# Q projection as a step of its own, a longer score queue and two-bank weight sharing in the down projection of a transformer layer

## The chip, the cores and the metric

The kernel runs on all 8 cores of one Trainium2 chip. Every core works alone on its own 1024 tokens; nothing is exchanged between cores. The metric is the device time of the slowest core, in microseconds (us). A change of less than about 2% either way is taken as no change.

## What is computed

The reference is one transformer layer on x of shape (2, 4096, 4096), cut here to what matters:

```python
xn = layernorm(x)
# multi-query attention: 32 query heads of 128, one shared key and value head, causal, ALiBi
q, k, v = split(xn @ Wqkv)            # q: 32 x 128, k: 128, v: 128
scores  = q @ k.T * 128**-0.5 + slope[h] * (pos_k - pos_q)     # causal
s = softmax(scores) @ v  @ Wo
# gated feed-forward with ternary weights, INTER = 11008
gate = (xn @ Wg.T) * ag
up   = (xn @ Wu.T) * au
out  = ((silu(gate) * up) @ Wd.T) * ad
return x + s * silu(out)
```

## The kernel before

Each core owns eight 128-token slots (`x_own`), chosen so that causal work is equal over the cores. Four stages follow each other, with a barrier of all engines between them (`b_p1`, `b_p2`, `b_p3`).

**Stage 1** normalizes all tokens that the core's queries can see, transposes them with TensorE, and keeps `xn` (own tokens, features on partitions), keys `ktsb` and values `vkm` in SBUF.

**Stage 2, attention.** The queries form two groups X = 0, 1 of four slots (512 tokens). For each head h and group X the keys are walked in tiles of 512 (8 tiles for X = 0, 7 for X = 1), each in two pairs of 128-key blocks. So a head has 30 steps, and a step has N = 512, 384, 256 or 128 query columns (causality removes slots from the later tiles). One step is:
- TensorE: two score products into the PSUM bank pair `2*pb, 2*pb+1` (L537; the pair alternates, and a step waits in `s_stepfree` until VectorE has emptied the pair of two steps earlier);
- VectorE: `usb = slope*rpsb + scores` (L744), which takes the ALiBi and mask term from the table `rpsb` in SBUF;
- ScalarE: `ptb = exp(usb)` (L891); `usb` and `ptb` have three buffers each;
- TensorE, later: two products with the values into an accumulator bank (L472) and two with a column of ones, which give the softmax sum in bank 5 (L478). `emit_attnv` issues these four; `ATT_LAG = 2` says that they are issued two steps behind the scores. They are called the PV products of a step below.

At the end of a group VectorE runs a tail: copy of the accumulator (L683), reciprocal of the sum row (L688), a cast (L691); TensorE later broadcasts the reciprocal with one matmul (L494), and VectorE multiplies (L699, L705), just ahead of the next group's tail. The sum bank is shared, so the first PV product of the next group waits for the reciprocal (`s_zev`). VectorE issues a tail after its work on the third step of the next group.

The query projection (32 chunks of the hidden dimension, weights `wqb` of one head) runs in halves of 512 tokens, `emit_qp_half`: both halves of heads 0 and 1 ahead of the loop, then the halves of head h+2 behind step 8 and step 22 of head h, into bank 7. VectorE copies them to `qtb`, which has two buffers (`emit_qtr`). GpSimd issues the load of the next head's `wqb` when both halves are done, and behind it two DRAM-to-DRAM casts of `Wd` and `Wo` to bfloat16 until all 48 are out. The table `rpsb` comes in four loads on SyncE's queue, and VectorE waits only for the chunk it needs.

**Stage 3** makes gate and up for 86 chunks of INTER; each explicit weight load serves two 512-column matmuls (L573 to L585). Results go to DRAM as `h_d`.

**Stage 4, down and output projection.** Tokens are in two blocks of 512 (`blk`), output columns in four blocks of 1024 (`o2`); oi counts these 8 blocks. In a block the half m = 0 (columns 0 to 511) runs through all 86 chunks of INTER with four token slots each into banks 0 to 3, then m = 1 into banks 4 to 7 (L616). The weights `wdb` come by GpSimd's queue in loads of 4 chunks x 512 columns (512 KB), two buffers per half; a load waits until the load two before it is used up. Then the output projection runs for jo = 0 into banks 0 to 3 and for jo = 1 into banks 4 to 7 (L630), with `wob` loads of 512 KB. VectorE and ScalarE finish each half: `gbuf` (L808), silu (L936), `sgb` (L819), residual add `oeb` (L828), store. VectorE's order is gbuf x4 of the half 0, sgb and oeb x4 of half 0, then the same for half 1. TensorE enters m = 0 of the next block when the first half's four banks are free, and m = 1 when the other four are.

Of the kernel before, what the change touches and what calls it, by code (L numbers as in the profile page):

```python
# [17 lines left out]
NLD = (IC + 3) // 4  # L18
# [8 lines left out]
NG = 15  # L27
# [60 lines left out]
M["usb"] = 176256  # L88
M["ptb"] = 188544
M["atstg"] = 194688  # L90
M["rzbsb"] = M["ag_t"]
assert M["atstg"] + 2048 <= 198624
# [44 lines left out]
def build_nc(dbg=False):  # L137
# [26 lines left out]
    def sb(name, shape, dt):  # L164
# [26 lines left out]
    qtb = sb("qtb", [128, 2, 1024], BF16)  # L191
# [11 lines left out]
            for i in range(4)]  # L203
# [19 lines left out]
                "b_p1", "s_rp", "s_wq", "s_stepdone", "s_stepfree", "s_qpmm", "s_qtr",  # L223
# [5 lines left out]
                "s_wdc", "s_wdc2", "s_woc", "s_dbgd", "s_cvt",  # L229
# [18 lines left out]
    NSH = 30  # L248
# [13 lines left out]
    with nc.Block() as block:  # L262

        @block.sync
        def _(q):
# [37 lines left out]
            for blk in range(2):  # L303
                if blk == 1:
                    q.wait_ge(SM["s_wdc"], 4 * IC)
                    q.wait_ge(SM["s_wdc2"], 4 * IC)
# [8 lines left out]
        def _(g):  # L315
# [22 lines left out]
            g.wait_ge(SM["s_kv"], 2 * NG)  # L338
            g.dma_start(wqb[:, :, :], wq4[0, :, :, :]).then_inc(SM["s_wq"], 16)
# [3 lines left out]
            for h in range(1, NH):  # L343
                g.wait_ge(SM["s_qpmm"], 2 * h)
# [30 lines left out]
            g.wait_ge(SM["s_cvt"], 16 * 48)  # L375
            woL = 0
            def _endicx(L):
                return (L // NLD) * IC + min(4 * (L % NLD) + 4, IC)
            for oi in range(8):
                blk, o2 = oi // 4, oi % 4  # L380
                for m in range(2):
                    cons = "s_wdc" if m == 0 else "s_wdc2"
                    for jj in range(NLD):
                        c = min(4, IC - 4 * jj)
                        L = oi * NLD + jj
                        if L >= 2:
                            g.wait_ge(SM[cons], _endicx(L - 2))
                        src = wdt_bf[4 * jj * 128:(4 * jj + c) * 128,
                                     o2 * 1024 + 512 * m:o2 * 1024 + 512 * m + 512
# [18 lines left out]
        def _(t):  # L408
# [44 lines left out]
            def emit_attnv(d):  # L453
# [5 lines left out]
                if first:  # L459
# [5 lines left out]
                    if g < 2:  # L465
                        t.wait_ge(SM["s_qtr"], 4)
# [558 lines left out]
```

## Time and profile before

| what | value |
|---|---|
| runs | 7837.72, 7880.9, 8567.01 us (median 7880.9) |
| profiled execution, whole | 7926.46 us |
| its span (slowest core, core 2) | 7924.9 us |
| spans of its eight cores | 7796.5 to 7924.9 us |
| TensorE busy | 6558.6 us (83%) |
| VectorE busy | 1948.4 us (25%) |
| ScalarE busy | 1222.4 us (15%) |
| DMA | 841.58 MB, mean 106 GB/s |

Busy shares are means over four stages with different limits. Matmuls are pipelined: a 512-column matmul is listed with 379 ns from start to end, while the next one starts long before that end, so busy times of single lines add up to more than the engine's. The profiled execution has two groups of cores: cores 0 to 3 share one die and ended at 7895 to 7925 us, cores 4 to 7 the other and ended at 7797 to 7831 us, at a higher granted TensorE clock.

### The profile page before, as it was taken

The numbers are of one execution on the slowest core, as the hardware profiler recorded it, in microseconds if no ns is written. First come the engines' busy times: TensorE is split into PE (matmuls) and PEld (weight loads), VectorE is DVE, ScalarE is ACT, GpSimd is POOL, SyncE is SP. The second block draws the span as 40 slices with busy tenths as digits, with TensorE's granted clock in tenths as the row PEclk, the third lists the DMA queues.
The fourth block names the chain that finished last, engine by engine and source line by source line (L and its number), as shares of the span: only waits on it lengthen the run. The fifth ranks groups of instructions, "written<-read, shape, count | busy, mean of one in ns | idle before, by whom it ended". The sixth has DMA issues, their size and how long they took to land.

```text
span 7924.9 us, 103467 instructions; the slowest of 8 cores (7796.5 to 7924.9 us)
## 1 busy us (share of the span) xinstructions
PE 6558.6 (83%) x29648; PEld 3574.2 (45%) x50512; DVE 1948.4 (25%) x2460; ACT 1222.4 (15%) x1931; POOL 533.2 (7%) x811
## 2 busy tenths in 40 slices
PE   4665657777777777999999999999677888888988
PEld 2333333444444333455555555555344544444544
DVE  5545525555555556000000000000000000000000
ACT  3333313333333333000000000000000000000000
POOL 0000000000000000000000000000111111111111
PEclk9666678888888888999999999999899987777877
DMA  5333388777755110444444444444443434433333
GB/s 181 149 128 138 138 129 110 109 109 108 105 87 85 21 21 12 85 91 85 81 86 86 90 86 85 85 85 86 159 134 122 134 127 162 139 126 115 124 127 116
DMA packets 244517, 841.58 MB, mean 106 GB/s; under 512 B 108306, under 2 KB 116516, under 8 KB 193360
## 3 DMA queue, kind: packets, MB, share of 16 engines
q0 software_dynamic: 113712, 658.76, 38.0%
q1 hardware_dynamic: 111904, 142.63, 5.8%
q10 hardware_dynamic: 18432, 33.56, 1.2%
q8 instruction: 340, 5.57, 0.3%
q14 instruction: 129, 1.06, 0.0%
HBM read 1126.93 MB, written 171.44 MB: 164 GB/s over the span
## 4 chain that ended last, share of the span: by engine, by line
PE 67%; DMA 14%; DVE 10%; issue 4%; ACT 4%; ACTq 0%; DVEq 0%; SPq 0%; POOL 0%; POOLq 0%
PE P L616 10%; DMA wdb<-wdt_bf 8%; PE P L574 8%; PE P L577 8%; PE P L585 7%; PE P L582 7%; PE P L507 6%; PE P L630 4%; PE P L472 4%; PE P L478 4%; PE P L537 3%; PE P L432 3%; DMA wob<-wo_bf 3%; DVE rzrow L688 3%; DVE usb L744 3%
## 5 line engine op out<-in xcount | busy, mean ns | idle before, releaser
L616 PE MATMUL P<-wdb,hblk 128*128 128x512 bf16 x5504 | 1400.9, 418 | 188.0 <-DMA wdb<-wdt_bf 144.4
L574 PE MATMUL P<-xn,wgb 128*128 128x512 bf16 x2752 | 1044.1, 379 | 12.0 <-DMA wub<-wu 12.0
L577 PE MATMUL P<-xn,wgb 128*128 128x512 bf16 x2752 | 1044.0, 379 | 0.0
L582 PE MATMUL P<-xn,wub 128*128 128x512 bf16 x2752 | 1043.0, 379 | 0.0
L585 PE MATMUL P<-xn,wub 128*128 128x512 bf16 x2752 | 1043.0, 379 | 0.0
L744 DVE SCALAR_TENSOR_TENSOR usb<-rpsb,P 128x768 f32<-128x768 f32 (+3 forms) x960 | 763.1, 795 | 874.9 <-PE P L537 740.6
L615 PEld LDWEIGHTS <-hblk 128*128 128x128 bf16 x5504 | 566.2, 105 | 811.9 <-issue 321.2
L891 ACT ACTIVATE ptb<-usb 128x768 bf16<-128x768 f32 (+3 forms) x960 | 686.5, 715 | 1447.7 <-DVE usb L744 1370.9
L472 PE MATMUL P<-ptb,vkm 128*128 128x128 bf16 (+3 forms) x1920 | 468.0, 328 | 423.5 <-DVE rzrow L688 400.2
L630 PE MATMUL P<-wob,atblk 128*128 128x512 bf16 x2048 | 546.7, 433 | 182.0 <-DVE gbuf L808 111.6
L417 PE MATMUL P<-I_bf,xntok 128*128 128x128 bf16 x2176 | 347.8, 265 | 384.5 <-DVE xntok L664 319.9
L783 DVE SCALAR_TENSOR_TENSOR hstg<-P,au_t,sgs 128x512 bf16<-128x512 f32 x86 | 64.6, 751 | 2271.3 <-ACT sgs L906 2271.3
L616 PEld LDWEIGHTS P<-wdb,hblk 128*128 128x128 bf16 x5504 | 519.8, 96 | 0.0
L507 PE MATMUL P<-xn,wqb 128*128 128x512 bf16 x2048 | 460.4, 384 | 58.0 <-DMA wqb<-wq 58.0
L537 PE MATMUL P<-qtb,ktsb 128*128 128x128 bf16 (+3 forms) x1920 | 441.0, 313 | 35.6 <-DVE usb L744 35.4
L417 PEld LDWEIGHTS P<-I_bf,xntok 128*128 128x128 bf16 x2176 | 225.4, 104 | 506.4 <-issue 461.5
L478 PE MATMUL P<-ptb,ones_bf 128*1 128x128 bf16 (+3 forms) x1920 | 441.7, 313 | 0.0
L573 PEld LDWEIGHTS <-wgb 128*128 128x128 bf16 x2752 | 269.5, 98 | 337.5 <-issue 13.5
L471 PEld LDWEIGHTS <-vkm 128*128 128x128 bf16 x1920 | 175.8, 102 | 544.8 <-issue 506.9
L581 PEld LDWEIGHTS <-wub 128*128 128x128 bf16 x2752 | 269.3, 98 | 324.7
L629 PEld LDWEIGHTS <-atblk 128*128 128x128 bf16 x2048 | 217.1, 108 | 431.3 <-issue 257.2
L903 ACT ACTIVATE sgs<-P,ag_t 128x512 f32<-128x512 f32 x86 | 59.2, 688 | 2239.4 <-PE P L585 2239.4
(76 smaller groups left out, 4947.3 us busy)
## 6 DMA issues: line engine op xcount, KB each, us to landing
wdb<-wdt_bf POOLq DMA_DIRECT2D x336, 512.0 KB, 3.8
wdt_bf<-wdt POOLq DMA_DIRECT2D x32, 2752.0 KB, 52.3
wgb<-wg POOLq DMA_DIRECT2D x86, 1024.0 KB, 8.4
wub<-wu POOLq DMA_DIRECT2D x86, 1024.0 KB, 12.8
wob<-wo_bf POOLq DMA_DIRECT2D x128, 512.0 KB, 4.2
xtile<-x_cov SPq DMA_DIRECT2D x60, 1024.0 KB, 5.4
xtile<-x_cov POOLq DMA_DIRECT2D x60, 1024.0 KB, 7.5
wqb<-wq POOLq DMA_DIRECT2D x32, 1024.0 KB, 12.1
```

The lines of the kernel that those rows point to most:

```text
L472: t.matmul(P[:, ab, co:co + N], vkm[:, (kcb + ci) * 128:(kcb + ci + 1) * 128], ptb[:, ub, j, 0:N], start=(first and j == 0), stop=(last an ...
L478: ins = t.matmul(P[0:1, 5, co:co + N], ones_bf[:, 0:1], ptb[:, ub, j, 0:N], start=(first and j == 0), stop=(last and j == 1))
L507: ins = t.matmul(P[:, bk, :], wqb[:, cc, :], xn[:, cc * 1024 + 512 * half: cc * 1024 + 512 * half + 512], start=(cc == 0), stop=(cc == HC ...
L537: ins = t.matmul(P[:, 2 * pb + j, 0:N], ktsb[:, kcol + ci * 128: kcol + (ci + 1) * 128], qtb[:, h % 2, qoff:qoff + N], start=True, stop=True)
L574: t.matmul(P[:, pg0, :], wgb[:, i % 2, cc, :], xn[:, cc * 1024:cc * 1024 + 512], start=(cc == 0), stop=(cc == HC - 1))
L577: t.matmul(P[:, pg1, :], wgb[:, i % 2, cc, :], xn[:, cc * 1024 + 512:(cc + 1) * 1024], start=(cc == 0), stop=(cc == HC - 1))
L582: t.matmul(P[:, pu0, :], wub[:, i % 2, cc, :], xn[:, cc * 1024:cc * 1024 + 512], start=(cc == 0), stop=(cc == HC - 1))
L585: ins = t.matmul(P[:, pu1, :], wub[:, i % 2, cc, :], xn[:, cc * 1024 + 512:(cc + 1) * 1024], start=(cc == 0), stop=(cc == HC - 1))
L616: ins = t.matmul(P[:, sl + 4 * m, :], hblk[sl][:, icx, :], wdb[:, slot, :], start=(icx == 0), stop=(icx == IC - 1))
L630: ins = t.matmul(P[:, sl + 4 * jo, :], atblk[:, hcx, sl * 128:(sl + 1) * 128], wob[:, slot, :], start=(hcx == 0), stop=(hcx == HC - 1))
L744: ins = v.scalar_tensor_tensor(usb[:, ub, :, 0:N], rpsb[:, o:o + 2 * N].rearrange("p (a b) -> p a b", b=N), float(SLOPES[h]), P[:, 2 * pb: ...
L891: ins = s.activation(ptb[:, ubp, :, 0:N], usb[:, ubu, :, 0:N], AF.Exp)
```

## The change

1. **Query projection.** It becomes a step ("qp", h) of the step list, ahead of each head's 30 steps. One explicit weight load serves both 512-column matmuls, into the bank pair of that step. VectorE empties both banks in one instruction into a single `qtb`; the first score step of the head waits for that. Heads 0 and 1 are no longer projected ahead, and no half stands inside a head. The first `wqb` load is issued behind the stage barrier, not ahead of it; the load of head h+1 is issued when the projection of head h is done.
2. **`ATT_LAG`** goes from 2 to 3; the broadcast matmul uses bank 7 and `rzbsb` gets its own place.
3. **`rpsb`** comes in one load, and VectorE waits for all of it before anything else of the stage.
4. **Down projection.** The loop over m is gone: one explicit weight load serves two matmuls (columns 0 to 511 and 512 to 1023), all eight banks are in use, and `wdb` loads hold 4 chunks x 1024 columns (1 MB), two buffers. A block starts when all eight banks of the block before are free. VectorE's order is unchanged.

The core of the diff:

```diff
+        steps.append(("qp", h))
...
-            for ck in range(4):
-                q.dma_start(rpsb[:, ck * 4608:(ck + 1) * 4608],
-                            rp[:, ck * 4608:(ck + 1) * 4608]
-                            ).then_inc(SM[f"s_wd{4 + ck}"], 16)
+            q.dma_start(rpsb[:], rp[:, :]).then_inc(SM["s_rp"], 16)
...
-            g.wait_ge(SM["s_kv"], 2 * NG)
-            g.dma_start(wqb[:, :, :], wq4[0, :, :, :]).then_inc(SM["s_wq"], 16)
             g.wait_ge(SM["s_xn"], NT)
             g.nop().then_inc(SM["b_p1"], 1)
             g.wait_ge(SM["b_p1"], 4)
-            for h in range(1, NH):
-                g.wait_ge(SM["s_qpmm"], 2 * h)
+            nsteph = 1 + 2 * (NKT[0] + NKT[1])
+            for h in range(NH):
+                if h >= 1:
+                    g.wait_ge(SM["s_stepdone"], nsteph * (h - 1) + 1)
                 g.dma_start(wqb[:, :, :], wq4[h, :, :, :]).then_inc(SM["s_wq"], 16)
...
+                for j in range((IC + 3) // 4):
+                    c = min(4, IC - 4 * j)
+                    t0 = 2 * IC * oi + 8 * j
+                    if oi > 0 and j < 2:
+                        g.wait_ge(SM["s_wdc"], 2 * IC * oi)
+                    elif j >= 2:
+                        g.wait_ge(SM["s_wdc"], t0 - 8)
+                    src = wdt_bf[4 * j * 128:(4 * j + c) * 128,
+                                 o2 * 1024:(o2 + 1) * 1024].rearrange(
+                                     "(a p) (m n) -> p a m n", p=128, n=512)
+                    g.dma_start(wdb[:, 8 * (j % 2):8 * (j % 2) + 2 * c, :]
+                                .rearrange("p (a m) n -> p a m n", m=2), src
+                                ).then_inc(SM[f"s_wd{wdL % 2}"], 16)
...
-            ATT_LAG = 2
+            ATT_LAG = 3
...
+                if stp[0] == "qp":
+                    h = stp[1]
+                    t.wait_ge(SM["s_wq"], 16 * (h + 1))
+                    for cc in range(HC):
+                        t.ldweights(wqb[:, cc, :])
+                        t.matmul(P[:, 2 * pb, :], wqb[:, cc, :],
+                                 xn[:, cc * 1024:cc * 1024 + 512],
+                                 start=(cc == 0), stop=(cc == HC - 1))
+                        ins = t.matmul(P[:, 2 * pb + 1, :], wqb[:, cc, :],
+                                       xn[:, cc * 1024 + 512:(cc + 1) * 1024],
+                                       start=(cc == 0), stop=(cc == HC - 1))
+                    ins.then_inc(SM["s_stepdone"], 1)
...
+                    if first and X == 0:
+                        t.wait_ge(SM["s_stepfree"], si)
...
-                for m in range(2):
-                    if oi == 0 and m == 0:
-                        t.wait_ge(SM["s_adb"], 8)
-                    if oi > 0:
-                        t.wait_ge(SM["s_gb"], (oi - 1) * 8 + 4 * (m + 1))
-                        t.wait_ge(SM["s_sgb"], (oi - 1) * 8 + 4 * (m + 1))
...
+                if oi == 0:
+                    t.wait_ge(SM["s_adb"], 8)
+                else:
+                    t.wait_ge(SM["s_gb"], oi * 8)
+                    t.wait_ge(SM["s_sgb"], oi * 8)
+                for icx in range(IC):
+                    L = oi * 22 + icx // 4
+                    slot = 8 * ((icx // 4) % 2) + 2 * (icx % 4)
+                    t.wait_ge(SM[f"s_wd{L % 2}"], 16 * (L // 2 + 1))
+                    for sl in range(4):
+                        t.ldweights(hblk[sl][:, icx, :])
+                        for j in (0, 1):
+                            ins = t.matmul(P[:, sl + 4 * j, :], hblk[sl][:, icx, :],
+                                           wdb[:, slot + j, :],
+                                           start=(icx == 0), stop=(icx == IC - 1))
...
+            v.wait_ge(SM["s_rp"], 16)
...
+                if stp[0] == "qp":
+                    h = stp[1]
+                    v.wait_ge(SM["s_stepdone"], si + 1)
+                    tv.wait_self(v)
+                    ins = v.tensor_scalar(
+                        qtb[:, :].rearrange("p (a b) -> p a b", a=2),
+                        P[:, 2 * (si % 2):2 * (si % 2) + 2, :],
+                        SCALE, None, ALU.mult)
+                    tv.inc(ins, SM, "s_stepfree", 1)
```

## Rows read from the trace of the kernel before

**Rows 1.** Span and mean granted TensorE clock of one core.

```profile
core 7: 7830.8 us, clock 0.908
```

**Rows 2.** Busy time by window, core 4: window, length, engines, clock, DMA share, GB/s.

```profile
3196.00:5560.00 2364.00, 2358.62 (x10929) 1283.90 (x16389) 121.25 (x172) 110.25 (x173) 88.90 (x168) 1.00 0.43 85
5628.00:7925.00 2297.00, 1715.45 (x7503) 1015.80 (x15002) 132.88 (x192) 40.40 (x64) 357.02 (x476) 0.96 0.38 128
```

**Rows 3.** Waits of core 4: who waited for whom, total us, times, longest.

```profile
PE P L472 <- DVE rzrow L688: 400.2, 63, 6.8
PE P L616 <- DMA wdb<-wdt_bf: 218.7, 187, 3.3
PE P L630 <- DVE gbuf L808: 111.1, 8, 14.5
```

**Rows 4.** Timeline of TensorE, core 4, start of attention: start, length, what, idle before.

```profile
1030.86 15.37 PE L507 MATMUL P<-xn,wqb 128*128 128x512 bf16 x64 [10.59 <-DMA wqb<-wq]
1063.28 16.21 PE L507 MATMUL P<-xn,wqb 128*128 128x512 bf16 x64 [17.05 <-DMA wqb<-wq]
...
1120.74 9.59 PE L507 MATMUL P<-xn,wqb 128*128 128x512 bf16 x32 [27.71 <-DMA wqb<-wq]
```

**Rows 5.** Timeline of TensorE, core 2, one head of attention.

```profile
2201.94 7.08 PE L507 MATMUL P<-xn,wqb 128*128 128x512 bf16 x32
...
2215.28 0.61 PE L537 MATMUL P<-qtb,ktsb 128*128 128x512 bf16 x2
...
2224.41 1.03 PE L472 MATMUL P<-ptb,vkm 128*128 128x512 bf16 x2 [6.29 <-DVE rzrow L688]
...
2231.59 0.50 PE L537 MATMUL P<-qtb,ktsb 128*128 128x384 bf16 x2
...
2232.81 0.50 PE L537 MATMUL P<-qtb,ktsb 128*128 128x384 bf16 x2
...
2248.89 0.60 PE L537 MATMUL P<-qtb,ktsb 128*128 128x512 bf16 x2
...
2258.45 1.04 PE L472 MATMUL P<-ptb,vkm 128*128 128x512 bf16 x2 [6.41 <-DVE rzrow L688]
...
2266.47 0.82 PE L507 MATMUL P<-xn,wqb 128*128 128x512 bf16 x3
```

**Rows 6.** Timeline of VectorE, core 2, in the same head.

```profile
2220.90 3.35 DVE L688 RECIPROCAL rzrow<-P 1x512 f32<-1x512 f32 x1
...
2225.66 1.22 DVE L744 SCALAR_TENSOR_TENSOR usb<-rpsb,P 128x1024 f32<-128x1024 f32 x1
```

**Rows 7.** Timeline of TensorE, core 4, down and output projection.

```profile
5613.73 9.07 PE L616 MATMUL P<-wdb,hblk 128*128 128x512 bf16 x32 [29.15 <-DMA atblk<-at_d]
5624.03 7.18 PE L616 MATMUL P<-wdb,hblk 128*128 128x512 bf16 x32 [1.24 <-DMA wdb<-wdt_bf]
5632.12 3.63 PE L616 MATMUL P<-wdb,hblk 128*128 128x512 bf16 x16 [0.91 <-DMA wdb<-wdt_bf]
...
5699.54 8.77 PE L616 MATMUL P<-wdb,hblk 128*128 128x512 bf16 x32 [1.98 <-DMA wdb<-wdt_bf]
...
5799.99 7.07 PE L630 MATMUL P<-wob,atblk 128*128 128x512 bf16 x32
...
6151.36 7.07 PE L616 MATMUL P<-wdb,hblk 128*128 128x512 bf16 x32
```

**Rows 8.** DMA issues, core 2: what, queue, count, KB each, median us to landing.

```profile
wdb<-wdt_bf POOLq DMA_DIRECT2D x336, 512.0 KB, 3.8
...
wdb<-wdt_bf POOLq DMA_DIRECT2D x16, 256.0 KB, 3.3
```

**Rows 9.** Timeline of VectorE, core 4, around the ends of projections.

```profile
5711.73 1.49 DVE L808 TENSOR_TENSOR gbuf<-P,adb 128x512 f32<-128x512 f32 x2 [0.15 <-DVE gbuf L808]
...
6156.67 0.69 DVE L819 SCALAR_TENSOR_TENSOR sgb<-P,g2buf 128x512 f32<-128x512 f32 x1
```

**Rows 10.** Timeline of TensorE, core 2, late in stage 4.

```profile
7041.39 8.58 PE L630 MATMUL P<-wob,atblk 128*128 128x512 bf16 x32 [1.19 <-DMA wob<-wo_bf]
```

More of the change, by code:

```diff
@@ L87 @@
 M["qtb"] = 172160
[L88 to L92, printed above, removed]
+M["usb"] = 174208
+M["ptb"] = 186496
+M["atstg"] = 192640
+M["rzbsb"] = 194688
+assert M["rzbsb"] + 2048 <= 198624
 M["wgb"] = 90240
@@ L190, in build_nc @@
     wqb = sb("wqb", [128, HC, 128], BF16)
-    qtb = sb("qtb", [128, 2, 1024], BF16)
+    qtb = sb("qtb", [128, 1024], BF16)
     usb = sb("usb", [128, 3, 2, 512], F32)
@@ L247, in build_nc @@
     NSTEP = len(steps)
-    NSH = 30
     pair_idx = {}
@@ L493, in emit_tail_mm @@
                     t.wait_ge(SM["s_rzb"], tg)
-                ins = t.matmul(P[:, 4 + 2 * (tg % 2), :], ones_bf[0:1, :],
-                               rzbf[0:1, tX, :], start=True, stop=True)
+                ins = t.matmul(P[:, 7, :], ones_bf[0:1, :], rzbf[0:1, tX, :],
+                               start=True, stop=True)
                 ins.then_inc(SM["s_rzmm"], 1)
@@ L498, in emit_tail_mm @@
                 return ins
-            def emit_qp_half(j, half):
-                t.wait_ge(SM["s_wq"], 16 * (j + 1))
-                if j >= 2:
-                    t.wait_ge(SM["s_qtr"], 2 * j + half)
-                bk = 7 if j >= 2 else (0, 1, 4, 5)[2 * j + half]
-                for cc in range(HC):
-                    t.ldweights(wqb[:, cc, :])
-                    ins = t.matmul(P[:, bk, :], wqb[:, cc, :],
-                                   xn[:, cc * 1024 + 512 * half:
-                                      cc * 1024 + 512 * half + 512],
-                                   start=(cc == 0), stop=(cc == HC - 1))
-                ins.then_inc(SM["s_qpmm"], 1)
-            for j in range(2):
-                for half in range(2):
-                    emit_qp_half(j, half)
             for si, stp in enumerate(steps):
@@ L534, in _ @@
-                for j in (0, 1):
-                    ci = 2 * pr + j
-                    t.ldweights(ktsb[:, kcol + ci * 128: kcol + (ci + 1) * 128])
-                    ins = t.matmul(P[:, 2 * pb + j, 0:N],
-                                   ktsb[:, kcol + ci * 128: kcol + (ci + 1) * 128],
-                                   qtb[:, h % 2, qoff:qoff + N],
-                                   start=True, stop=True)
-                ins.then_inc(SM["s_stepdone"], 1)
-                if tail is not None and si > tail_armed + 8:
-                    emit_tail_mm()
@@ new lines, in _ @@
+            for si, stp in enumerate(steps):
+                if stp[0] == "qp":
[7 more added lines that the diff above has]
+                    tv.inc(ins, SM, "s_stepfree", 1)
+                else:
+                    _, h, X, kt, pr = stp
+                    lo, ns = CFG[X][kt]
+                    N = ns * 128
+                    first = (kt == 0 and pr == 0)
+                    last = (kt == NKT[X] - 1 and pr == 1)
+                    pb = si % 2
+                    ub = pr_cnt2 % 3
+                    o = RP_OFF[(X, kt)] + 2 * pr * N
+                    v.wait_ge(SM["s_stepdone"], si + 1)
+                    if pr_cnt2 >= 3:
+                        v.wait_ge(SM["s_pt"], pr_cnt2 - 2)
+                    tv.wait_self(v)
+                    ins = v.scalar_tensor_tensor(
+                        usb[:, ub, :, 0:N],
+                        rpsb[:, o:o + 2 * N].rearrange("p (a b) -> p a b", b=N),
+                        float(SLOPES[h]), P[:, 2 * pb:2 * pb + 2, 0:N],
+                        ALU.mult, ALU.add)
+                    tv.inc(ins, SM, "s_stepfree", 1)
+                    pr_cnt2 += 1
+                    if last:
+                        pend_t.append((h, X, pair_idx[(h, X, kt, pr)]))
+                    while pend_t and pend_t[0][2] + 2 < pr_cnt2:
+                        while pend_t2:
+                            emit_tail_v2(pend_t2.pop(0))
+                        emit_tail_v(pend_t.pop(0))
```

142 lines of the change are left out of this document (38 added, 104 removed).

## The prediction

> **What bounds the kernel now.** I read the spans of the cores first. The slowest core of the profile (core 2, 7924.9 us) is on a die with a lower TensorE clock; the slowest of the other die ends at 7830.8 [rows 1]. Most rows below are of core 4, on that second die. The windows by stage come next [rows 2]. Stage 3 has it busy without a gap, at clock 1.00: 2364 us for 86 x 128 = 11008 matmuls, 0.2148 us each. The change does not touch stage 3. Stage 4 has 1715 of 2297 us busy. VectorE is busy for 133 and ScalarE for 40 of these, so TensorE's work plus its waits make this stage. In attention VectorE matters too, by one chain in each group, shown below. The waits [rows 3] name them: in attention 63 waits for the reciprocal, in stage 4 187 waits for `wdb` and 8 for `gbuf`. A listed wait begins only at the modelled end of the last matmul, about 0.16 us after its last column, so the true gaps are longer; below I take starts from the timelines.
>
> **Start of attention.** Stage 1 ends at 1020.3 on core 4 (the first wait of [rows 4] counts back to it). Before: two projections, then the first score at 1079.3, that is 59.0 us (the second projection, 16.21 us less 0.16 of the last matmul's drain, ends there); then 27.7 us of waiting for `wqb` of head 2 [rows 4]. After: `wqb` of head 0 is issued about 1 us later than stage 1 ends, beside the 9.4 MB of `rpsb` and two casts. Nearest row: the second `wqb` load, issued at the end of the first projection (1046.8) beside the same traffic, let TensorE start at 1063.3, 16.5 us later. So the projection starts near 1038 and ends near 1054. VectorE then waits for all of `rpsb`. Its four loads had landed 39 us after their issue before, with the casts beside them only for the last third; I take 50 us, so the first score is at about 1072: 52 us. The bounds are 42 us (as fast as before, then one eviction) and 67 us (twice as slow as alone). `wqb` of head 1 is issued at 1054 and needed about 64 us later; the slowest one took 40.4 us before. The 27.7 us wait goes. Sum: 59.0 + 27.7 against 52.
>
> **A head of attention.** Before, 64.5 us (2201.94 to 2266.47, [rows 5]). Its parts:
> - two halves of the projection, 32 x 0.2162 = 6.92 us each;
> - twice the chain from the first score of a new group to its first PV product, 2215.28 to 2224.41 = 9.1 us and 2248.89 to 2258.45 = 9.6 us. VectorE sets it: two score evictions of 1.22, the multiply of the group before, the copy, the reciprocal of 3.35 [rows 6];
> - what lies between: 2224.41 to 2248.89 less a half = 17.6 us, and the other 14.4 us.
>
> After:
> - The projection is one block of 64 matmuls in stage 3's pattern, 64 x 0.2148 = 13.75 us, against 13.84.
> - Nothing hides the eviction of `qtb`: the next score waits for it. A 1024-column eviction took 1.22 us [rows 6]; with semaphores 1.5 us. It is bounded by 1.4, and by 3.2 if the clock drops behind the gap (32 matmuls took 8.77 instead of 7.1 us behind a 1.98 us gap, [rows 7]). VectorE loses two copies of 0.69 in exchange, one of which stood in the chain of 9.6; that chain becomes 9.1.
> - The chain itself stays: VectorE's list in it is the same. But TensorE does one more score product and one more old PV step in its shadow, because the queue is one deeper. I added up the stretch between two chains by columns: 512 columns take 0.2148 us, so the six products of a step take 0.97 us at N = 384, and a step without a wait took 2231.59 to 2232.81 = 1.22 us [rows 5], 0.25 more for changing weights. That makes a PV step 1.1, 0.9, 0.7 and 0.5 us and a score pair 0.4, 0.3, 0.2 and 0.1 us for N = 512, 384, 256, 128, plus 1.9 us because the first products behind the chain run at half speed (1.03 us for two, against 0.60). The part of 17.6 us becomes 15.6, that of 14.4 becomes 12.7. About half of this is the step in the shadow, the other half the small waits of TensorE for `ptb` at N = 128, where the scores of two steps ago are barely through VectorE and ScalarE when they are wanted.
> - Could a third pending step hurt? `ptb` has three buffers, so exp of step n waits for PV of n-3, which is issued right behind score n and ends before VectorE is through with score n. No.
>
> Head after: 15.6 + 9.1 + 12.7 + 13.75 + 1.5 + 9.0 = 61.7 us, 2.8 less. If the deeper queue brings nothing it is 65.4. The last two heads had no projection before, one fewer is inside the stage now. Whole stage before: 59.0 + 27.7 + 60 x 6.92 + 32 x 50.7 = 2124 us. After: 52 + 32 x 46.4 + 31 x 15.25 = 2010. **Attention: -114 us** (bounds -124, with the first score 42 us behind stage 1, and +15, with 67 us and the 65.4 us head).
>
> The loads for the casts keep their place: a pair of casts and one `wqb` fill most of the DMA time of a head, and there is about 45 us of slack for `wqb`.
>
> **Down projection.** A block's L616 part on core 4 lasts from 5613.73 to 5799.99 = 186.3 us [rows 7]; the eight add up to 1464. The products alone would take 688 x 0.2148 = 147.8 us. The difference is the `wdb` wait. 16 matmuls use up a load in 3.46 us, but the next into that buffer needs 0.7 us to be issued and 3.9 us to land: 4.6 us. So every second load is late: 5624.03 to 5632.12 is 8.1 us for 32 matmuls. After, a load of 1 MB serves 32 matmuls, 6.9 us. Its landing time is not in the trace. From 256 to 512 KB it rose from 3.3 to 3.8 [rows 8]; two more such steps give 4.8 to 5.1 us, and with 0.8 us for the issue 5.9 us, under 6.9. Upper bound: twice 3.9, then each turn is 8.6 us and 64 matmuls take 15.5 us, where they took 16.2. I take the first, with 4 us in a block for the clock behind its start and for a late load: 152 us. **-248 us** (bounds -265 and -60).
>
> The Trainium skill (DMA: Bandwidth & Descriptors, Anatomy of one DMA) puts a transfer from GpSimd's queue at about 2.0 us plus its bytes at 436 GB/s. By it, as an estimate, doubling 512 KB adds 1.2 us, which is what the two sizes of [rows 8] give too; nothing in the sum rests on it.
>
> What the eight shared banks cost:
> - jo = 0 must wait until banks 0 to 3 are emptied, which lay under m = 1 before. Four `gbuf` take 2 x 1.49 + 0.15 = 3.13 us [rows 9]; the first can start about 1.2 us ahead of the last matmul's end, so 2 us remain, 3 with the clock. 8 x 3 = +24 us.
> - The next block must wait for the fourth `sgb` of jo = 1. TensorE moved on at 6151.36 before [rows 7], that `sgb` ended at 6156.67 + 0.69 = 6157.36 [rows 9]: +6.0 us, 6.3 with the semaphores, at 7 boundaries, one of which already waits 14 us for `atblk`. 6 x 6.3 = +38 us.
> - The 14 us wait ahead of jo = 1 (111 us in all) stays: VectorE still does sgb and oeb of half 0 first.
>
> **Down and output projection: -186 us.**
>
> **Sum.** -114 - 186 = -300. On the second die 7830.8 + 1.6 becomes 7532. On core 2 the last five blocks run at a lower clock (32 matmuls in 8.58 us, 0.268 each, [rows 10]); its waits for `wdb` are shorter, so it gains 98 + 51 instead of 248 there, and 7926.5 becomes about 7725. The median of the runs, 7880.9, is 49 us above the first of these bases. I forecast the undisturbed case with a part of that excess: 7570 us.
>
> **Rivals.**
> - *The denser stage 4 draws a lower clock on both dies.* For it: core 2 did its last blocks at 0.268 us per matmul on the same work. Against: stage 3 is denser than anything in stage 4 and had clock 1.00, core 4 kept 0.96. Price: 8 x (184.4 + 4) = 1507 instead of 1216 us (+291), and the output projection's turns 8.9 instead of 8.1 us for 32 matmuls, 64 of them (+50). 7532 + 341 = 7870: no change. Chance 0.15. The Trainium skill (TensorE: Matmul & The Clock Gate, The HAM clock gate) states a limit that can hold a whole die at 13/16 of the full clock, which speaks for this rival. The trace agrees in size on core 2 (0.2148 / 0.268 = 0.80) and not in stage 3, where core 4 had 1.00 [rows 2].
> - *The 1 MB loads are late too.* At the upper bound -60 instead of -248: 7570 + 188 = 7760. For it: landings scatter, one wait was 3.3 us. Chance 0.09.
> - *The deeper queue brings nothing*, because VectorE's chain decides. Then the head is 65.4 us and attention is unchanged: 7570 + 115 = 7685. Chance 0.12.
> - *Slower: the serial projection starves VectorE and ScalarE.* If with the queue drained each head refilled so slowly that the time behind the projection grew, the loss would be 31 times that. To end 2% above 7880.9 it must eat 458 us, 14.8 us a head; the whole chain of a new group is 9.1 us and is in my sum. Chance 0.04.
>
> **Chances.** Forecast 0.60. Range: its own 7480 to 7660; up to 7790 it takes in the idle queue and the late loads, and part of the lower clock. Faster by over 2% (below 7723): the forecast, the idle queue, and a third of the late loads, 0.75; same 0.20; slower 0.05. Two per cent is about what a measurement of this kernel can tell from no change.
>
> **What would show it.** Waits for `wdb` fall from 219 [rows 3] to under 50 us; the L616 part of a block is near 152 us; TensorE waits about 6 us at seven block starts and 2 us ahead of jo = 0; a head takes 62 us, with a 1.5 us gap behind 64 projection matmuls; the first score is near 1072. The forecast falls if a 1 MB load needs over 7 us from buffer free to landed, or if the clock in stage 4 is near 0.8 on all cores.

## The result, and the profile after

| what | value |
|---|---|
| kernel after, median of 10 runs | 7609.78 us (7588.80 to 8129.08) |
| kernel before, median of its 10 runs beside them | 8361.5 us (7837.72 to 8579.37) |
| ratio after to before | 0.9667, interval 0.9629 to 0.9705 |
| profiled execution, whole | 7610.64 us |
| forecast, as a ratio | 7570 / 7880.9 = 0.9605 |

The median of before is high because in many of its runs the cores of a die were held at a lower TensorE clock; the ratio leaves such runs of both kernels out, and everything below goes by it. Of the kernel before it rests on two times only, 7837.72 and 7880.9 us. So the change gives 3.3%, some 260 us of 7837.72, and not the 752 us between the medians. I had forecast 3.9%, just outside the interval. The time itself is 40 us above the forecast.

The spans by core of the kernel after (its slowest core is 0 now, and the granted clocks of the two dies agree; [rows 1] of before is core 7):

```profile
core 0: 7609.1 us, clock 0.897
...
core 3: 7527.4 us, clock 0.904
core 4: 7568.4 us, clock 0.901
...
core 7: 7596.3 us, clock 0.898
```

Windows of core 4, with the columns of [rows 2]: a stretch of stage 3, and stage 4.

```profile
3160.00:5520.00 2360.00, 2348.57 (x10882) 1278.44 (x16320) 121.22 (x172) 110.23 (x173) 90.97 (x171) 1.00 0.44 85
5569.00:7568.00 1999.00, 1706.36 (x7552) 934.80 (x12352) 132.87 (x192) 40.37 (x64) 226.53 (x302) 0.94 0.43 148
```

Waits of core 4, and the last line of core 0 (who waited for whom, total, times, longest):

```profile
PE P L464 <- DVE rzrow L673: 332.4, 63, 11.6
PE P L615 <- DVE gbuf L781: 124.3, 16, 14.6
PE P L615 <- DMA wob<-wo_bf: 99.0, 60, 12.4
PE P L526 <- DVE qtb L699: 64.4, 32, 15.9
PE P L601 <- DVE sgb L792: 53.2, 7, 15.4
...
DVE atstg L668 <- DMA at_d<-atstg: 16.8, 3, 6.6
PE P L601 <- DMA wdb<-wdt_bf: 6.1, 9, 1.1
```

```profile
DVE atstg L668 <- DMA at_d<-atstg: 47.7, 10, 8.7
```

Three things against [rows 3]. The 218.7 us of waiting for `wdb` are 6.1. The wait for the reciprocal fell from 400.2 to 332.4, though its longest rose from 6.8 to 11.6. And there is a wait that before did not have: VectorE's copy into `atstg` waits for the store of an earlier attention output. It is 47.7 us on core 0 and 6.0 on core 3, and the order of the eight cores by this wait (3, 5, 2, 4, 6, 1, 7, 0) is their order by span. The spans differ by 82 us and the waits by 42, so the wait is not all that sets them apart.

From the last transpose of stage 1 to the end of the last `usb`, core 4 took 2130.2 us before and takes 2079.4 now; core 0 takes 2113.4, core 3 2062.3. So **attention gave 51 us on core 4**, where I had written 114. From the first product of the down projection to the last of the output projection core 4 took 2173.8 us and takes 1989.9: **184 us**, where I had written 186.

The start of attention on TensorE and VectorE (timelines of core 4; compare [rows 4]):

```profile
1023.64 0.38 PE L433 MATMUL P<-I_bf,vtstg 128*128 128x128 bf16 x4 [1.58 <-ACT vtstg L842]
1053.92 0.61 PE L502 MATMUL P<-xn,wqb 128*128 128x512 bf16 x1 [29.90 <-DMA wqb<-wq]
```

```profile
1084.75 1.23 DVE L699 TENSOR_SCALAR qtb<-P 128x1024 bf16<-128x1024 f32 x1 [86.99 <-DMA rpsb<-rp]
```

The first projection starts 30 us behind the last transpose and is over by 1067.7; `rpsb` is all there only at 1084.75, so `rpsb` alone sets the start. A head in the middle of attention (TensorE, then VectorE, core 4; compare [rows 5, 6]):

```profile
2044.91 0.60 PE L526 MATMUL P<-qtb,ktsb 128*128 128x512 bf16 x2 [1.56 <-DVE qtb L699]
...
2054.04 1.03 PE L464 MATMUL P<-ptb,vkm 128*128 128x512 bf16 x2 [4.97 <-DVE rzrow L673]
...
2070.40 0.60 PE L526 MATMUL P<-qtb,ktsb 128*128 128x512 bf16 x2
...
2079.54 1.03 PE L464 MATMUL P<-ptb,vkm 128*128 128x512 bf16 x2 [5.08 <-DVE rzrow L673]
...
2092.27 0.39 PE L502 MATMUL P<-xn,wqb 128*128 128x512 bf16 x1
...
2107.82 0.61 PE L526 MATMUL P<-qtb,ktsb 128*128 128x512 bf16 x2 [1.56 <-DVE qtb L699]
...
2116.95 1.03 PE L464 MATMUL P<-ptb,vkm 128*128 128x512 bf16 x2 [4.97 <-DVE rzrow L673]
...
2132.60 0.60 PE L526 MATMUL P<-qtb,ktsb 128*128 128x512 bf16 x2
...
2141.83 1.03 PE L464 MATMUL P<-ptb,vkm 128*128 128x512 bf16 x2 [5.17 <-DVE rzrow L673]
...
2155.71 0.39 PE L502 MATMUL P<-xn,wqb 128*128 128x512 bf16 x1
```

```profile
2106.43 1.23 DVE L699 TENSOR_SCALAR qtb<-P 128x1024 bf16<-128x1024 f32 x1 [13.79 <-PE P L505]
```

In the order of the forecast this head is 9.13 + 16.36 + 9.14 + 12.73 + 13.75 + 1.80 = 62.9 us, and the next one 63.4.

A block of stage 4 (TensorE, core 4; compare [rows 7]):

```profile
5970.65 7.08 PE L615 MATMUL P<-wob,atblk 128*128 128x512 bf16 x32 [2.19 <-DVE gbuf L781]
...
6018.40 8.63 PE L615 MATMUL P<-wob,atblk 128*128 128x512 bf16 x32 [12.88 <-DVE gbuf L781]
...
6060.86 16.49 PE L601 MATMUL P<-wdb,hblk 128*128 128x512 bf16 x64 [6.52 <-DVE sgb L792]
```

The L601 part of this block had begun at 5814.71 and its products ended near 5968.3: 153.6 us. The eight parts of core 4 take 150.2 to 153.7 us, 152.1 on average, where those of before took 180 to 189, 183 on average. From this block's start to the next it is 246.1 us.

### The profile page after: what moved, and what is told of

It is laid out like the page before. It is cut to its first block, busy times and chain, and to the rows that moved or that the text cites. A ratio compares the mean times of both kernels' runs of the same rounds, so it can differ in the third digit from the quotient of the medians.

```text
span 7609.1 us, 97882 instructions; the slowest of 8 cores (7527.4 to 7609.1 us)
## 1 busy us (share of the span) xinstructions
PE 6257.2 (82%) x29119; PEld 3394.6 (45%) x46736; DVE 1943.1 (26%) x2428; ACT 1222.2 (16%) x1931; POOL 399.8 (5%) x635
## 4 chain that ended last, share of the span: by engine, by line
PE 72%; DMA 10%; DVE 9%; issue 4%; ACT 3%; another core or an unknown queue 1%; ACTq 0%; DVEq 0%; SPq 0%; POOL 0%; POOLq 0%
PE P L601 15%; PE P L562 8%; PE P L570 8%; PE P L559 8%; PE P L567 7%; PE P L615 4%; DMA at_d<-atstg 4%; PE P L470 4%; PE P L526 3%; PE P L464 3%; PE P L427 3%; DMA wob<-wo_bf 3%; PE P L505 3%; PE P L412 3%; PE P L502 3%
## 5 line engine op out<-in xcount | busy, mean ns | idle before, releaser
L601 PE MATMUL P<-wdb,hblk 128*128 128x512 bf16 x5394 | 1201.9, 382 | 97.2 <-DVE sgb L792 55.3
L562 PE MATMUL P<-xn,wgb 128*128 128x512 bf16 x2752 | 1044.3, 379 | 17.1 <-DMA wub<-wu 11.3
L570 PE MATMUL P<-xn,wub 128*128 128x512 bf16 x2752 | 1043.0, 379 | 5.8
L559 PE MATMUL P<-xn,wgb 128*128 128x512 bf16 x2642 | 1002.4, 379 | 0.0
L567 PE MATMUL P<-xn,wub 128*128 128x512 bf16 x2641 | 1000.9, 379 | 0.0
L615 PE MATMUL P<-wob,atblk 128*128 128x512 bf16 x2007 | 489.7, 401 | 234.6 <-DVE gbuf L781 127.4
L601 PEld LDWEIGHTS P<-wdb,hblk 128*128 128x128 bf16 x5504 | 531.4, 97 | 217.9 <-issue 7.6
L599 PEld LDWEIGHTS <-hblk 128*128 128x128 bf16 x2752 | 271.1, 99 | 434.1 <-issue 119.2
L558 PEld LDWEIGHTS <-wgb 128*128 128x128 bf16 x2752 | 269.3, 98 | 336.8 <-issue 12.6
L505 PE MATMUL P<-xn,wqb 128*128 128x512 bf16 x1024 | 389.6, 380 | 8.0 <-issue 6.3
L502 PE MATMUL P<-xn,wqb 128*128 128x512 bf16 x961 | 365.8, 381 | 29.5 <-DMA wqb<-wq 29.5
## 6 DMA issues: line engine op xcount, KB each, us to landing
wub<-wu POOLq DMA_DIRECT2D x86, 1024.0 KB, 13.5
```

Source lines behind the costliest of these rows:

```text
L559: t.matmul(P[:, pg0, :], wgb[:, i % 2, cc, :], xn[:, cc * 1024:cc * 1024 + 512], start=(cc == 0), stop=(cc == HC - 1))
L562: t.matmul(P[:, pg1, :], wgb[:, i % 2, cc, :], xn[:, cc * 1024 + 512:(cc + 1) * 1024], start=(cc == 0), stop=(cc == HC - 1))
L567: t.matmul(P[:, pu0, :], wub[:, i % 2, cc, :], xn[:, cc * 1024:cc * 1024 + 512], start=(cc == 0), stop=(cc == HC - 1))
L570: ins = t.matmul(P[:, pu1, :], wub[:, i % 2, cc, :], xn[:, cc * 1024 + 512:(cc + 1) * 1024], start=(cc == 0), stop=(cc == HC - 1))
L601: ins = t.matmul(P[:, sl + 4 * j, :], hblk[sl][:, icx, :], wdb[:, slot + j, :], start=(icx == 0), stop=(icx == IC - 1))
L615: ins = t.matmul(P[:, sl + 4 * jo, :], atblk[:, hcx, sl * 128:(sl + 1) * 128], wob[:, slot, :], start=(hcx == 0), stop=(hcx == HC - 1))
```

## The experiments

My theory on the result: the down projection did what was forecast, since a load now serves 6.9 us of products instead of 3.46; attention gained less because the first loads collide with the casts, because the half-speed stretch behind each chain is longer than I had allowed, and because the stores of the attention outputs are late. The main rivals: the gain of stage 4 comes from something other than the loads (half as many weight changes, say), and the longer queue does nothing.

**The two halves of the change alone.** `e1_down` is the kernel before with the new down projection only, `e2_att` the kernel before with the new attention only.

> The kernel before with only the down projection changed (shared weight loads, eight banks, 1 MB loads). If the gain of the change is mostly there, as the traces say (core 4: 2173.8 to 1989.9 us for this stage), this gains about 184 us, ratio about 0.977, and its attention stage takes as long as before. If the two parts help each other (a shorter attention stage shifting the clock or the memory traffic of the last stage), it gains clearly less than 184 us.

> The kernel before with only the attention stage changed. Forecast from the prediction: -114 us. From the trace of the changed kernel: about -50 us on core 4, and less on the cores where the stores of at_d come late. Ratio about 0.993 to 0.997. Down projection blocks stay at 180 to 186 us for their L616 part.

Down alone: 0.9815 (0.9649 to 0.9982), the fastest run 7636.91 us against 7827.79 of the kernel before beside it; waits for `wdb` 13.5 us. The interval is wide, but the rows say the same as above:

```profile
6152.39 97.87 PE L615 MATMUL P<-wdb,hblk 128*128 128x512 bf16 x439 [6.14 <-DVE sgb L818]
6306.19 7.08 PE L629 MATMUL P<-wob,atblk 128*128 128x512 bf16 x32 [2.19 <-DVE gbuf L807]
```

153.8 us from one to the other. Attention alone: 0.994 (0.9892 to 0.9988), that is 47 us of 7830. With intervals this wide the two ratios cannot show that the halves leave each other alone; the stages of core 4 can. The down and output projection takes 1990.0 us in `e1_down` and 1989.9 in the kernel after, 2177.4 in `e2_att` and 2173.8 before. Attention takes 2082 us in `e2_att` against 2079 after, and 2139 in `e1_down` against 2130 before. So neither half helps or harms the other by more than 9 us, and the missing part of the forecast is attention's.

**Is it the size of the loads?** `e7_small` is the kernel after with loads of 512 KB (two chunks of 1024 columns) into two buffers. Weight changes, banks and order stay those of after.

```
-                for j in range((IC + 3) // 4):       # loads of 4 chunks, 1 MB
+                for j in range(IC // 2):             # loads of 2 chunks, 512 KB
-                    slot = 8 * ((icx // 4) % 2) + 2 * (icx % 4)
+                    slot = 4 * (L % 2) + 2 * (icx % 2)
```

> The changed kernel with down loads of 2 chunks x 1024 columns (512 KB, two buffers of that size) in place of 1 MB; the shared weight loads and the eight banks stay. If the size of what two buffers hold is what the change gained, every second load is late again: 8.1 us for 32 matmuls, the L601 part of a block goes from 153.6 back to about 180 us and the kernel is 200 to 230 us slower. If sharing the weight loads is the gain (rival), the part stays near 155 us.

Measured: 1.0068 (1.0039 to 1.0097) to the kernel before. From core 4's waits and timeline of TensorE:

```profile
PE P L600 <- DMA wdb<-wdt_bf: 249.7, 226, 3.6
```

```profile
5855.98 9.30 PE L600 MATMUL P<-wdb,hblk 128*128 128x512 bf16 x32 [6.11 <-DVE sgb L791]
...
6041.50 8.71 PE L614 MATMUL P<-wob,atblk 128*128 128x512 bf16 x32 [2.20 <-DVE gbuf L780]
```

The part of this block is 183.3 us again, and that is the shortest of the eight: they take 183.3 to 193.5 us, 189 on average, against 183 before and 152 after. So the size of what the two buffers hold is what the change gained, and the loss is larger than the 200 to 230 us that I had expected: the stage takes 2274.7 us on core 4, 285 more than in the kernel after and 101 more than before. Of these 101, 55 are the two bank waits of the rows, which the forecast had booked, and 51 are parts that are 6 us longer than those of before, with loads of the same size and the same turn; why, no run here shows. 101 less attention's 47 (2082.5 against 2129.9 us) is the loss of 0.7%. Sharing the explicit weight loads gives no time where loads are late; what it could give where none is late, the next run shows.

**Or the depth?** `e8_ring` is the kernel before, half by half, 512 KB loads, but its 2 + 2 buffers used as one ring of four.

```
-                        g.dma_start(wdb[:, 8 * m + 4 * (L % 2):
-                                        8 * m + 4 * (L % 2) + c, :], src
-                                    ).then_inc(SM[f"s_wd{2 * m + L % 2}"], 16)
+                        g.dma_start(wdb[:, 4 * (R % 4):4 * (R % 4) + c, :], src
+                                    ).then_inc(SM[f"s_wd{R % 4}"], 16)
```

> The kernel before with its 512 KB loads, its half after half order and the same 16 KB of wdb a partition, but as one ring of four buffers instead of two for each half, so that a load has three loads' time (10.4 us) instead of one (3.46 us). By the theory that a load is late because of its turn of 4.6 us and not because of its size, the L616 part of a block falls from 182 to about 150 us with no wait for shared banks: -250 us, ratio about 0.968. If small loads are themselves the limit (rival), it stays above 170 us.

Measured: 0.9651 (0.962 to 0.9681). No wait for `wdb` is left in the list, and the part is 148.5 us long in six of the eight blocks and 150 to 151 in the two behind the waits for `atblk` (timeline of TensorE, core 0):

```profile
6076.27 148.66 PE L618 MATMUL P<-wdb,hblk 128*128 128x512 bf16 x688
6224.77 7.07 PE L632 MATMUL P<-wob,atblk 128*128 128x512 bf16 x32
```

688 x 0.2148 is 147.8, so TensorE is full here, with an explicit weight load for every single matmul. By the rate of stage 3, sharing one between two could take off 0.7 us a block at most, and the rival on weight changes falls. (The profile also lists a weight load inside each matmul: stage 4 has 15002 of both kinds for 7503 matmuls in [rows 2] and 12352 for 7552 now, so sharing removed a quarter of those of the down projection and not half.) The median landing of a load was 4.3 us (core 0), longer than the 3.8 of [rows 8], and did no harm. The wait of before came from this: of its four buffers only two were in turn, so a freed one had the 3.46 us of the other to be filled again, where issue and landing need 4.6. In the ring it has three times 3.46. These few lines give as much as the whole change, without its two bank waits.

**The first loads of attention.** `e6_start` is the kernel after with `wqb` of head 0 loaded ahead of stage 1's end and `rpsb` in four loads, as before.

```
+            g.wait_ge(SM["s_kv"], 2 * NG)
+            g.dma_start(wqb[:, :, :], wq4[0, :, :, :]).then_inc(SM["s_wq"], 16)
             g.wait_ge(SM["s_xn"], NT)
-            q.dma_start(rpsb[:], rp[:, :]).then_inc(SM["s_rp"], 16)
+            for ck in range(4):
+                q.dma_start(rpsb[:, ck * 4608:(ck + 1) * 4608], ...)
```

> The changed kernel with the start of attention as before: the first wqb load issued ahead of the barrier and rpsb in four loads, of which VectorE waits for the one it needs. In the changed kernel the first score came 62.6 us behind stage 1 on core 4 (the prediction had 52). If the two late loads are the cause, the first score comes at 27 to 35 us and the kernel gains 25 to 30 us. If the casts set the pace of the first heads (rival), the second wqb load comes late in its turn and less than 10 us are left.

On core 4 (last transpose at 1024.64), TensorE and VectorE:

```profile
1037.28 0.61 PE L510 MATMUL P<-xn,wqb 128*128 128x512 bf16 x1 [12.26 <-DMA wqb<-wq]
```

```profile
1055.58 5.20 DVE L730 SCALAR_TENSOR_TENSOR usb<-rpsb,P 128x1024 f32<-128x1024 f32 x4 [0.95 <-PE P L534]
```

The first `usb` comes 31 us behind the last transpose instead of 63; the projection, which starts 12.6 us behind it, sets that now, and no longer `rpsb`. The fastest run took 7553.27 us against 7588.8 of the kernel after: 35 us. That is without an interval, but the rows show 32 of them, and attention on core 4 takes 2045.5 us instead of 2079.4.

**The queue's length.** `e3_lag2` is the kernel after with ATT_LAG 2, `e4_lag3` the kernel before with ATT_LAG 3: one number each.

> The changed kernel with ATT_LAG 2 again. If the deeper queue brings what the prediction said (about 3.7 us a head without it), a head goes from 63.1 to about 66 to 67 us and the kernel is 90 to 120 us slower, so that the serial projection alone would have cost time. If VectorE's chain alone sets a head (rival), nothing changes: under 10 us.

> The kernel before with ATT_LAG 3 alone. By the prediction's walk along the queue a head goes from 64.5 to about 61 us, -100 us in all. If VectorE's chain alone sets a head (rival), under 10 us. If late stores of at_d matter, they show here only weakly, because the halves of the projection stand inside each group and leave 30 us or more between two tails.

`e3_lag2`: heads of 66.85 us on core 4 against 63.15, attention 2174 us against 2079, its wait for the reciprocal 399.3 us, as long as before. Its fastest run took 7692.40 us, 104 more than the fastest of the kernel after, without an interval:

```profile
PE P L464 <- DVE rzrow L673: 399.3, 63, 6.7
```

So the third pending step is worth 3.7 us a head here, exactly the difference of the forecast's 65.4 and 61.7; the rival "the deeper queue brings nothing" falls. `e4_lag3`: 0.9942 (0.9913 to 0.9971), heads of 63.85 against 64.8, attention on core 4 2092 us against 2130. I had expected heads of 61 us and -100 us in all, and that did not come, though the wait for the reciprocal fell by 84 us,

```profile
PE P L472 <- DVE rzrow L688: 316.6, 63, 5.4
```

which is as much as in the kernel after when its 16.8 us of late stores are left out. Only 1.0 us of a head came of it. What took the rest can be read in one place of core 4, TensorE:

```profile
2192.99 1.03 PE L472 MATMUL P<-ptb,vkm 128*128 128x512 bf16 x2 [4.97 <-DVE rzrow L688]
2195.64 0.82 PE L537 MATMUL P<-qtb,ktsb 128*128 128x384 bf16 x2 [0.67 <-DVE usb L744]
```

Behind the chain TensorE waits again, for a `usb` that VectorE had put behind a copy of `qtb`. That it explains all of the 2.7 us is argued, not shown. A serial projection with ATT_LAG 2 (`e3_lag2`) takes 66.85 us, 2 us more than before; so the serial projection by itself costs time, and the queue pays for it.

**The late stores.** `e5_at4b` is the kernel after with four staging buffers and semaphores for the outputs instead of two.

```
-    atstg = sb("atstg", [128, 2, 512], BF16)
+    atstg = sb("atstg", [128, 4, 512], BF16)
-                if tg >= 2:
-                    v.wait_ge(SM[f"s_atsp{tX}"], 16 * (tg // 2))
+                if tg >= 4:
+                    v.wait_ge(SM[f"s_atsp{tg % 4}"], 16 * (tg // 4))
```

> The kernel after, with four staging buffers and semaphores for the attention outputs instead of two, so that the copy into atstg no longer waits for the store of two tails ago. In the kernel after this wait was 6.0 us (core 3) to 47.7 us (core 0) in the profiled run. My theory: the late stores lengthened the heads directly, so the wait goes on all cores, the first copy to last reciprocal time of core 0 falls from that of the kernel after towards that of core 3, last transpose to last usb is about 2062 us on every core (core 0 had 2113.4), and the slowest core is 45 to 55 us shorter, 7555 to 7565 us. Rival: the stores are late because the DMA queues are full of casts, and what waits for those moves the stall to another place (the load of the stored output, the next head's weights): heads of core 0 stay at 69 to 72 us in that stretch, and the time stays within 10 us of the kernel after.

In the kernel after the wait acts like this (core 4, VectorE, then TensorE):

```profile
1498.77 0.69 DVE L668 CAST atstg<-P 128x512 bf16<-128x512 f32 x1 [6.59 <-DMA at_d<-atstg]
```

```profile
1471.78 1.03 PE L464 MATMUL P<-ptb,vkm 128*128 128x512 bf16 x2 [4.97 <-DVE rzrow L673]
1503.08 1.03 PE L464 MATMUL P<-ptb,vkm 128*128 128x512 bf16 x2 [11.57 <-DVE rzrow L673]
```

The 6.6 us go into the chain as they are: 4.97 becomes 11.57. The store that this copy waits for was issued just before the copy of the tail ahead (core 4, the queue of SyncE; its landing is timed in the same trace at 31.1 us):

```profile
1467.44 0.32 SPq L278 DMA_DIRECT2D at_d<-atstg  x1
```

From this issue the copy had 25.4 us. All 3 waits of core 4 and all 10 of core 0 are for stores of group X = 0, which must land between the tail of X = 1 and that of the next X = 0. With four buffers the wait is gone, though the stores landed no sooner (median 22.1 us on core 0, 16.4 in the kernel after). Core 0 takes 2059.6 us from last transpose to last `usb` instead of 2113.4, core 4 2057.6 instead of 2079.4 (some 6 us of both are an earlier first score: `rpsb` landed in 53.7 us in this run, not 59.6); the heads of core 0 in that stretch fall from 69 to 73 us to 62 to 64. The slowest core of the profiled run is 7565.2 against 7609.1. The ratio to the kernel before, 0.9661 (0.9633 to 0.9689), cannot tell it from the kernel after, because the times of before that it uses are lower too (7822.47 to 7835.85 us, against 7837.72 and 7880.9). The times themselves, 7560.48 to 7566.7 us against 7588.80 to 7610.64, and the views of the cores show the gain.

**The wait ahead of jo = 1.** `e9_order` is `e8_ring` with VectorE making `gbuf` for both halves before the first `sgb`, ScalarE's silus in the same order, and eight `g2buf` buffers.

> The ring of four buffers, and VectorE takes gbuf of both halves before sgb and oeb of either (silu results in eight buffers, in the place of adrow). The 14 us wait ahead of jo = 1, which both kernels have eight times, should go: another 110 to 125 us, ratio about 0.953 in all. If TensorE is then held by something else at that place (wob loads, the next block's banks), less than 60 us.

The `gbuf` wait is gone, but cores 0 to 3 end at 7422 to 7477 us, about 72 us below those of `e8_ring` (7508 to 7548) and not 110; its fastest run took 7485.71 us against 7552.23. The wait for `wob` rose from 89.8 us (61 times) to 131.4 (78 times), both on core 0 (the two expectations below say core 4). Part of it had lain under the `gbuf` wait.

**All that helped, together.** `e10_best` is the attention of after with the cures of `e6_start` and `e5_at4b`, and the down projection of `e9_order`. `e11_wob3` gives the weights of the output projection three buffers instead of two.

> Attention of the kernel after with four staging buffers, the early load of the first head's weights and the row of scales in four loads; down projection half by half as before, with a ring of four 512 KB buffers and both halves' gbuf work ahead on VectorE. If the parts add up: start of attention 31 us behind the last transpose instead of 62.6 (-31), no staging wait (-45 on the slowest core), ring instead of two large buffers and gbuf ahead (7420 to 7480 against 7526 to 7550 of the ring alone, about -72). From 7610 of the kernel after: about 7400 to 7430 us, a ratio of 0.94 to 0.945 to the kernel before. Rival: the ring's and the attention's gains fall on the same DMA queues and collide (wob loads late, at least 131 us of waits for them on core 4 as in the run with the new order), and the time is above 7470.

> The kernel of e10_best with three buffers instead of two for the output projection's weights (wob). With two, TensorE waited 131 us for wob loads in 78 places on core 4 once gbuf was ahead. Theory: as with wdb, the turn of two buffers (issue, wait for release, landing) is longer than the matmuls that one buffer feeds, and a third takes the wait away: from 131 us to under 20, and the time about 80 to 110 us below e10_best, near 7300 us. Rival: the wob loads are late since the DMA engines are taken by other transfers of this stage, so the wait falls by less than 30 us and the time by less than 30.

`e10_best`: 0.9436 (0.9396 to 0.9477), as expected; its fastest runs, 7384.95 and 7390.59 us, lie a little below the expected 7400 to 7430, so the gains add up and the rival falls. `e11_wob3`: fastest run 7237.11 us, where the fastest of before beside it took 7822.47: 0.925, without an interval. Waits of `e10_best` (core 0), then of `e11_wob3` (core 4):

```profile
PE P L627 <- DMA wob<-wo_bf: 146.0, 80, 14.2
```

```profile
PE P L627 <- DMA wob<-wo_bf: 25.5, 16, 10.9
```

Blocks of `e11_wob3`, TensorE, core 4:

```profile
6807.42 148.66 PE L613 MATMUL P<-wdb,hblk 128*128 128x512 bf16 x688
6955.91 45.22 PE L627 MATMUL P<-wob,atblk 128*128 128x512 bf16 x208
7002.15 10.53 PE L627 MATMUL P<-wob,atblk 128*128 128x512 bf16 x48 [1.02 <-DMA wob<-wo_bf]
7012.52 0.81 PE L613 MATMUL P<-wdb,hblk 128*128 128x512 bf16 x3
```

A block takes 205.1 us, and its 944 products alone 944 x 0.2148 = 202.8. It was 225.0 in `e10_best`. The gain is 153 us for the stage (1838.9 us on core 0 of `e10_best`, 1685.7 on core 4 here) and 148 between the fastest runs. It is more than the 80 to 110 I had expected and than the 120 us of listed waiting, since behind such a wait the first products run slower too: in the kernel after, 32 of them took 8.77 us behind a `wob` wait of 2.14 us and 7.08 without a slow start. How much of the remaining 30 us that makes was not separated. The rival (the engines are taken by other transfers) falls: the median landing of a `wob` load on core 4 is 5.2 us with three buffers and was 4.6 with two in `e10_best`; it is later, and waited for less.

## Why the prediction was half right

- **Down projection: right, term by term.** Part of a block 152.1 us on average (forecast 152); turn of a 1 MB load: it lands in 5.4 us (forecast 4.8 to 5.1) and is under the 6.9 us of its products, wait 6.1 us in all (forecast under 50); bank wait ahead of jo = 0 2.2 us (2 to 3); block starts 6.1 to 6.7 us (6.3), and 15.4 at the one that waits for `atblk` too; the wait ahead of jo = 1 stays, 12.9 in the row above (14). Sum -184 against -186. `e7_small` and `e8_ring` show that the cause was named rightly too. The Trainium skill (DMA: Bandwidth & Descriptors, Anatomy of one DMA) would put the 1 MB load at 2.0 us and 1 MB at 436 GB/s, 4.4 us as an estimate; the trace has 5.4. From 512 KB to 1 MB the landing grew by 1.5 us (3.9 to 5.4), not by the 1.0 that the two sizes of [rows 8] give; with 0.8 us for the issue the turn is 6.2, still under 6.9.
- **Attention: the step that failed,** -51 instead of -114 on core 4. The stage took 2079 us and not 2010. Two sizes in its sum were too small, the start and the stretches behind the chains, and one wait was put at nothing, that for the stores of the outputs. Its parts:
  - *Start.* "I take 50 us, so the first score is at about 1072: 52 us." The first score was 62.5 us behind the last transpose, 10.5 more. `rpsb` landed in 59.6 us, and that sets it. `wqb` let TensorE start after 30 us and not 17.7, but the projection was over 17 us before `rpsb` came, so this error cost nothing. That the casts beside `rpsb` make the 9.6 us is argued: no run has the one load without them. The upper bound, 67, held it.
  - *Head.* 63.15 us on average instead of 61.7, 46 us in 32 heads. The two chains (9.13, 9.14) and the projection (13.75) were right. The eviction gap is 1.8, not 1.5. The rest lies behind the chains: 16.36 + 12.73 = 29.1 us in one head and 29.5 in the next, for a forecast of 15.6 + 12.7 = 28.3. I had allowed 1.9 us behind each chain for products at half speed. In each of the two heads that fits one stretch, 12.73 in the first and 15.65 in the second (2116.95 to 2132.60): TensorE is slow for 3.3 us at its start. The other stretch, slow for 4.8 or 5.8 us, is 0.8 or 1.2 us too long.
  - *Stores.* "The loads for the casts keep their place ... about 45 us of slack" looked at the loads alone. The stores of the outputs go out beside the casts, and each must land between one tail and the next. In the kernel before, those of X = 0 needed 27.2 to 32.4 us on core 4 in the heads with casts, where the last stores of the stage, without casts, need 1.7, and they had 34.1 us or more; those of X = 1 had 30.6 us and mostly needed 10 or less. The old kernel hid the former by 2 us. With all of the projection on one side of a head, the tails of X = 1 and of the next X = 0 are 25.4 us apart and the other two 38, so the time of the slow stores shrank by 9 us. They need 17 to 31 us now, and do not always fit. On core 4 that is 17 us, on core 0 48, and since the time is the slowest core's it is core 0 that counts.
  
  10.5 + 46 + 17 = 74, and the stage is 69 over the forecast; the 5 us between them are not assigned. One bound was added up wrongly too: 67 us and the 65.4 us head give +19, not +15. The measured -51 lies inside it either way.
- **The rivals.** "The 1 MB loads are late too" did not come. "The deeper queue brings nothing" is refuted by `e3_lag2`. "The serial projection starves VectorE": by itself it costs 2 us a head, far from what it would have needed (14.8 in the text, 15.1 when 468 us, from 7570 to 2% above 7880.9, are shared by 31). "The denser stage 4 draws a lower clock": stage 4 of core 4 has 0.94 against 0.96 of [rows 2], and the slowest part of 688 products took 153.7 us, not the 184.4 of that rival. It did not come in the execution that was profiled.
- **The base.** I had added 38 us to the sum (7532 to 7570) for the median of the runs of before. The runs that the ratio compares took 7588.8 to 7610.6, so this margin covered a part of attention's miss, by luck.

## What to carry to other kernels

Two buffers are enough only if issue and landing of a load take less than the products of **one** load; otherwise first count the buffers that are really in turn: one ring of four instead of two pairs gave 3.5% without more memory and without another matmul order. When work is moved inside a loop, measure the new distance between any two users of one buffer, stores included, since a cover that shrinks from 34.3 to 25.4 us turns a store that was hidden by 2 us into a wait in the critical chain; pair each buffer's users one by one, because the medians of both groups together (9.6 us of landing) hid this. Each removed wait uncovers the next one on the same engine (`gbuf`, then `wob`); look for it in the same list before counting the gain.

## What the runs showed of the hardware

How long TensorE stays at the lower of its two levels behind a gap varies, with nearly the same gap in front. Timeline of TensorE, kernel after, core 4, behind the gap of 5.08 us and behind that of 5.17 us a head later:

```profile
2082.10 0.85 PE L464 MATMUL P<-ptb,vkm 128*128 128x512 bf16 x2
2082.88 0.59 PE L470 MATMUL P<-ptb,ones_bf 128*1 128x512 bf16 x2
```

```profile
2144.39 1.06 PE L464 MATMUL P<-ptb,vkm 128*128 128x512 bf16 x2
2145.39 1.01 PE L470 MATMUL P<-ptb,ones_bf 128*1 128x512 bf16 x2
```

Two matmuls of 512 columns take about 1.03 us at 1.2 GHz and 0.60 at 2.4. The full level is back about 3 us behind the chain in the first case and over 5 in the second; the granted clock of the two stretches up to the projection is 0.88 and 0.79, and the second is 1.1 us longer. On cores 3 and 4 this stretch, from the chain of X = 1 to the projection, alternates from head to head: 12.7 to 12.8 us in one and 13.8 to 14.0 in the next, with few exceptions. What decides it, no run here shows.

A load's landing time says little about whether it is waited for: `wdb` loads of 512 KB landed in 3.9 us before (median, core 4) and were late 187 times, in 4.3 us in the ring of four (core 0) and were never late.
